# Router logits of 13 tiles as GpSimd products and ScalarE sums, all queries made with 512 columns in the normalisation stage

## The reference

```python
h = layernorm(x)
q, k, v = h @ W_q.T + b_q, h @ W_k.T + b_k, h @ W_v.T + b_v
z = (q @ k.T) / sqrt(512) * adj
z = where(z == 0, -10000, z)
x = x + relu(softmax(z, axis=1) @ v)
X = layernorm(x)
router_w = softmax(X @ Wr)                # Wr: 512 x 8
topk_w, topk_idx = top_k(router_w, 2)     # two of eight experts, weights softmax(topk_w)
x = x + swiglu(X, shared) + sum over the two experts of weight * swiglu(X, expert)
```

## Time and profile before

| | |
|---|---|
| time, median of 3 runs | 1431.06 us (1430.62 to 1432.37) |
| the profiled execution | 1431.42 us, its span 1429.3 us |
| granted TensorE clock, mean | 0.998 |
| TensorE (PE) busy | 1417.1 us, 99% |
| VectorE (DVE) busy | 672.1 us, 47% |
| ScalarE (ACT) busy | 438.1 us, 31% |
| GpSimd (POOL) busy | 188.9 us, 13% |

### The profile page before, as it was taken

The page is one execution under the profiler, slowest core; times in us unless marked ns, Lnnn a source line. Parts: engine busy times, 40 slices in busy tenths (PEclk is TensorE's granted clock), DMA queues, the critical chain, the costliest instruction groups (busy, mean ns, idle before and its releaser), DMA issues.

```text
span 1429.3 us, 19916 instructions
## 1 busy us (share of the span) xinstructions
PE 1417.1 (99%) x7140; PEld 1224.3 (86%) x7140; DVE 672.1 (47%) x1425; ACT 438.1 (31%) x705; POOL 188.9 (13%) x233
## 2 busy tenths in 40 slices
PE   8999999999999999999999999999999999999999
PEld 6788888888888888898999889898898989888887
DVE  4955656665666577543253425234152525242222
ACT  3521121222111235343243424234242525231211
POOL 1510111121112133011001010101101010100000
PEclk9999999999999999999999999999999999999999
DMA  4811222232213256272617134251435262621000
GB/s 145 247 58 65 99 72 73 73 99 85 81 66 118 73 178 235 89 213 54 197 31 214 29 74 156 44 200 34 117 109 151 78 160 86 183 88 60 0 30 30
DMA packets 81666, 149.81 MB, mean 105 GB/s; under 512 B 10464, under 2 KB 20704, under 8 KB 79536
## 3 DMA queue, kind: packets, MB, share of 16 engines
q1 hardware_dynamic: 65312, 117.76, 23.9%
q0 software_dynamic: 9760, 18.93, 6.7%
q10 hardware_dynamic: 6528, 12.22, 3.1%
HBM read 109.90 MB, written 40.04 MB: 105 GB/s over the span
## 4 chain that ended last, share of the span: by engine, by line
PE 98%; DVE 1%; DMA 0%; SPq 0%; issue 0%; POOL 0%; ACT 0%; DVEq 0%; POOLq 0%
PE bank L234 92%; PE bank L667 2%; PE bank L690 1%; PE bank L871 1%; PE bank L820 1%; PE bank L684 0%; DMA wk_raw<-in_L_gnn_W_k_dram 0%; PE bank L827 0%; PE bank L620 0%; PE bank L604 0%; SPq L312 0%; DVE y L1546 0%; PE bank L698 0%; PE bank L636 0%; DVE xn L1197 0%
## 5 line engine op out<-in xcount | busy, mean ns | idle before, releaser
L1514 DVE TENSOR_TENSOR hid<-bank,hid 128x384 f32<-128x384 f32 (+1 forms) x96 | 57.8, 602 | 355.6 <-PE bank L234 355.6
L234 PE MATMUL bank<-dn_h,hT_h 128*128 128x512 f32 x416 | 167.1, 402 | 0.3 <-DVE hT_l L1185 0.3
L234 PE MATMUL bank<-dn_h,hT_l 128*128 128x512 f32 x416 | 163.2, 392 | 0.0
L234 PE MATMUL bank<-dn_l,hT_h 128*128 128x512 f32 x416 | 162.8, 391 | 0.0
L234 PE MATMUL bank<-xq_h,gate_h 128*128 128x384 f32 (+1 forms) x384 | 136.2, 355 | 0.1
L234 PE MATMUL bank<-xq_h,gate_l 128*128 128x384 f32 (+1 forms) x384 | 136.1, 354 | 0.0
L234 PE MATMUL bank<-xq_l,gate_h 128*128 128x384 f32 (+1 forms) x384 | 135.7, 353 | 0.0
L234 PE MATMUL bank<-xq_h,up_h 128*128 128x384 f32 (+1 forms) x384 | 135.6, 353 | 0.0
L234 PE MATMUL bank<-xq_h,up_l 128*128 128x384 f32 (+1 forms) x384 | 135.4, 353 | 0.0
L234 PE MATMUL bank<-xq_l,up_h 128*128 128x384 f32 (+1 forms) x384 | 135.3, 352 | 0.0
L1089 ACT ACTIVATE hid<-bank 128x384 f32<-128x384 f32 (+1 forms) x96 | 50.7, 528 | 224.0 <-PE bank L234 224.0
(11 more groups left out here) (214 smaller groups left out, 2791.1 us busy)
## 6 DMA issues: line engine op xcount, KB each, us to landing
adj_t<-in_adj_dram SPq DMA_DIRECT2D x16, 1024.0 KB
gate_raw<-in_L_ffn_Wg_dram SPq DMA_DIRECT2D x16, 1024.0 KB, 5.4
up_raw<-in_L_ffn_Wu_dram SPq DMA_DIRECT2D x16, 1024.0 KB, 9.1
dn_raw<-in_L_ffn_Wd_dram SPq DMA_DIRECT2D x16, 1024.0 KB, 11.3
x_t<-in_x_dram SPq DMA_DIRECT2D x24, 256.0 KB, 4.3
slots<-x2row ACTq DMA_DIRECT2D x12, 512.0 KB, 4.3
e_x<-slots ACTq DMA_DIRECT2D x22, 256.0 KB, 2.7
acc<-x SPq DMA_DIRECT2D x16, 256.0 KB
```

What stands on the lines that cost most here:

```text
L234: mm = pe.matmul(o, lhs(a, c), rhs(b, c), start=first and n == 1, stop=last and n == 3 * len(chunks))
L1514: dve.tensor_tensor(hid[:, c % 2, 0:w], bank[2 + c % 2][:, 0:w], hid[:, c % 2, 0:w], ALU.mult).then_inc(sem("hid"), 1)
```

## The change

- The queries of all tiles are made in the normalisation stage, from its fourth tile on and during the first scores, in 16 blocks with 512 columns (`queries(q)`). ScalarE adds the bias (`keep_queries`; the scale is put into A), SyncE stores each to DRAM (`store_queries`), and in the loop the queries of the next pair are fetched in two halves into one tile `y_f` (`load_queries`), from which ScalarE and VectorE make the two parts. The second half is fetched when the first has been read.
- The router logits of tiles 1 to 13 (`BY_ROWS`) are made from the normalised row itself: for each expert GpSimd multiplies the row by a row of the transposed router weights (`products`, two buffers), and ScalarE sums the product (`sum_products`). The last three tiles use TensorE as before. The transposed weights are made by one DMA with single numbers as its pieces (`wrt`) near the start, and spread over all partitions later (`wr_rows`).
- The order within a step changes: the turned row behind the third score block, the count of picks one step later and behind the first score block, `pick_weights` and `ranks` of the tile before behind the second fill, `logits` behind the second half of the queries.
- adj is loaded in two halves; `sc` keeps eight pieces of 512 columns, which the two tiles use in turn; `x1`, `y_f` and others lie at new addresses. The last two steps are written out on their own (`step_before_last`, `last_step`).
- ScalarE's second SiLU of the experts waits until all rows of x1 are stored. Calls of `wait` with a positive value become direct `wait_ge`, and the setup semaphores are joined in one.

```diff
+    y_all = nc.dram_tensor("y_all", [T // 2, DC * 256], F32, kind="Internal").ap()
+    wrt = nc.dram_tensor("wrt", [E, D], F32, kind="Internal").ap()
...
-sc = at("sc", 168 * K, [P, 2, T])
+sc = at("sc", 168 * K, [P, 8 * 512])
+prod = at("prod", 180 * K, [P, 2, D])
+wr_rows = at("wr_rows", 128 * K, [P, E, D])
+y_new = at("y_new", 152 * K, [P, 2, 512])
 fill = at("fill", 184 * K, [P, 512])
-y_f = at("y_f", 186 * K, [P, 2, 256])
+y_f = at("y_f", 192 * K, [P, 2, 256])
 x_t = at("x_t", 188 * K, [P, 2, D])
-x1 = at("x1", 192 * K, [P, D])
+x1 = at("x1", 186 * K, [P, D])
...
+BY_ROWS = NT - 3
+def place(b, n, final=False):
+    return (4 + n if final or n < 2 else n) if b else n
+def whole(b, final=False):
+    return slice(place(b, 0, final) * 512, (place(b, 0, final) + 4) * 512) if final or not b else slice(1024, 3072)
 def queries_follow(j, b):
     return b == 0 and (not isinstance(j, int) or j + 1 < NT // 2)
+def logits_follow(i):
+    return not isinstance(i, int) or 1 <= i <= BY_ROWS
...
+    sp.dma_start(wrt, w_r.rearrange("d e -> e d"), allow_slow_non_contiguous=True).then_inc(sem("in_wr"), 16)
...
+    def store_queries(q):
+        g, m = q // 4, q % 4
+        sp.wait_ge(sem("y_kept"), q + 1)
+        sp.dma_start(y_all[2 * g * P:2 * (g + 1) * P, m * 256:(m + 1) * 256].rearrange("(a p) q -> p a q", p=P),
+                     y_new[:, q % 2, :].rearrange("p (a q) -> p a q", a=2)).then_inc(sem(f"y_out{q % 2}"), 16)
+    def load_queries(j, half):
+        wait(sp, "yT_l", 2 * j + half)
+        sp.dma_start(y_f[:], rows(y_all, j)[:, half * 512:(half + 1) * 512].rearrange("p (c q) -> p c q", c=2)
+                     ).then_inc(sem("y_in"), 16)
+    def load_adj(i, half):
+        wait(sp, "scored", 4 * i - 2 + 2 * half)
+        sp.dma_start(adj_t[:, half * 1024:(half + 1) * 1024], rows(adj, i)[:, half * 1024:(half + 1) * 1024]
+                     ).then_inc(sem(f"adj_in{half}"), 16)
     for t in range(4, NT):
         wait(sp, "ln1_done", t - 3)
         load_x(t)
-    wait(sp, "wv_turned", DC)
-    sp.dma_start(adj_t[:], rows(adj, 0)).then_inc(sem("adj_in"), 16)
+        if t >= 10:
+            store_queries(t - 10)
+    sp.wait_ge(sem("wv_turned"), DC)
+    load_adj(0, 0)
+    load_adj(0, 1)
...
+    load_queries(0, 0)
+    store_queries(6)
+    store_queries(7)
+    load_queries(0, 1)
+    for q in range(8, 16):
+        store_queries(q)
+    load_adj(1, 0)
+    sp.wait_ge(sem("y_kept"), 16)
+    sp.wait_ge(sem("in_wr"), 32)
+    sp.dma_start(wr_rows[:].rearrange("p e d -> p (e d)"),
+                 wrt.rearrange("(a e) d -> a (e d)", a=1).broadcast_to([P, E * D])).then_inc(sem("in_wr"), 16)
+    for half in range(2):
+        sp.wait_ge(sem(f"y_out{half}"), 16 * 8)
...
+    def store_row(i):
+        sp.wait_ge(sem("x1_done"), i + 1)
         sp.dma_start(rows(acc, i), x1[:]).then_inc(sem("x1_out"), 16)
-        wait(sp, "x2T_done", i + 1)
+    def store_turned(i):
+        sp.wait_ge(sem("x2T_done"), i + 1)
         sp.dma_start(rows(x2t, i), x2T[:].rearrange("p c q -> p (c q)")).then_inc(sem("x2t_out"), 16)
-    fetch(0, 0)
-    fetch(1, 1)
-    store(0)
+    def serve(j, b):
+        i = 2 * j + b
+        load_adj(i + 1, 1)
+        fetch(i, b)
+        ahead = queries_follow(j, b)
+        if ahead:
+            load_queries(j + 1, 0)
+        if not isinstance(i, int) or i > 0:
+            store_row(i - 1)
+        if not isinstance(i, int) or i + 2 < NT:
+            load_adj(i + 2, 0)
+        if not isinstance(i, int) or i > 0:
+            store_turned(i - 1)
+        if ahead:
+            load_queries(j + 1, 1)
+    serve(0, 0)
+    serve(0, 1)
     with sp.Fori(1, NT // 2 - 1) as j:
         for b in range(2):
-            fetch(2 * j + b, b)
-            store(2 * j + b - 1)
-    fetch(NT - 2, 0)
-    store(NT - 3)
+            serve(j, b)
...
+    serve(NT // 2 - 1, 0)
...
+    store_row(NT - 2)
+    store_turned(NT - 2)
+    sp.wait_ge(sem("attended"), 4 * NT)
     load_unit(1)
+    store_row(NT - 1)
     wait(sp, "xq_l", prepared(0))
-    wait(sp, "w_l", 2)
+    sp.wait_ge(sem("w_l"), 2)
     load_unit(2)
-    store(NT - 1)
...
+    def products(n, b):
+        wait_apart(pool, "x2_done", n)
+        for e in range(E):
+            wait_apart(pool, f"logit_sum{e % 2}", 4 * (n - 1) + e // 2)
+            pool.tensor_tensor(prod[:, e % 2, :], x2row[b][:], wr_rows[:, e, :], ALU.mult).then_inc(sem("products"), 1)
     power_of_row(1, 0)
+    pool.wait_ge(sem("in_wr"), 48)
+    products(1, 0)
     power_of_row(2, 1)
+    products(2, 1)
     scatter(1, 0)
-    with pool.Fori(1, NT // 2) as j:
+    with pool.Fori(1, BY_ROWS // 2) as j:
         power_of_row(2 * j + 1, 0)
+        products(2 * j + 1, 0)
         scatter(2 * j, 1)
         power_of_row(2 * j + 2, 1)
+        products(2 * j + 2, 1)
         scatter(2 * j + 1, 0)
+    power_of_row(BY_ROWS, 0)
+    products(BY_ROWS, 0)
+    scatter(BY_ROWS - 1, 1)
+    for n in range(BY_ROWS + 1, NT + 1):
+        power_of_row(n, (n - 1) % 2)
+        scatter(n - 1, n % 2)
...
-    def queries(j, half):
-        for c in range(2):
-            m = 2 * half + c
-            mm = product(pe, bank[7][:, c * 256:(c + 1) * 256], lambda a, d: A[a][:, d, m * P:(m + 1) * P],
-                         lambda b, d: xnT[b][:, d, bass.ds(j * 256, 256)], range(DC))
-        mm.then_inc(sem("y_ps"), 1)
+    def queries(q):
+        g, m = q // 4, q % 4
+        pe.wait_ge(sem("A_done"), DC)
+        pe.wait_ge(sem("xnT_l"), 4 * g + 4)
+        wait(pe, "y_kept", q - 1)
+        product(pe, bank[4 + q % 2][:], lambda a, d: A[a][:, d, m * P:(m + 1) * P],
+                lambda b, d: xnT[b][:, d, g * 512:(g + 1) * 512], range(DC)).then_inc(sem("y_ps"), 1)
...
-    def attention_step(j, b, last=False, prev=True, split=False):
+    def attention_step(j, b):
         i = 2 * j + b
...
+        prev = not isinstance(i, int) or i > 0
         if b == 1:
             wait(pe, "yT_l", 2 * j + 4)
         scores(i + 1, 1 - b, 0)
+        if not isinstance(i, int) or i > 1:
+            count_picks(i - 1)
         scores(i + 1, 1 - b, 1)
         turn(i, b, 0)
         turn(i, b, 1)
+        scores(i + 1, 1 - b, 2)
         if prev:
             turn_normalised(i, b)
-        scores(i + 1, 1 - b, 2)
-        if prev:
-            route_logits(i)
         scores(i + 1, 1 - b, 3)
-        ahead = queries_follow(j, b)
-        if ahead:
-            if prev:
-                wait(pe, "logits_read", i)
-            queries(j + 1, 0)
         attend(i, 0)
         turn(i, b, 2)
         attend(i, 1)
-        if ahead:
-            wait(pe, "yT_f", 2 * j + 3)
-            queries(j + 1, 1)
         turn(i, b, 3)
         attend(i, 2)
-        if split:
-            turn(i + 1, 1 - b, 0)
         attend(i, 3)
...
+        if t >= 3:
+            queries(t - 3)
         values(t)
...
+        act.wait_ge(sem("y_in"), 16 * n + 16)
+        wait(act, "scores", 4 * n if half == 0 else 4 * n - 4)
         copy(yT["h"][:, 2 * half:2 * half + 2, :], y_f[:]).then_inc(sem("yT_h"), 1)
...
+    def keep_queries(q):
+        act.wait_ge(sem("y_ps"), q + 1)
+        act.wait_ge(sem("bias_read"), 3)
+        wait(act, f"y_out{q % 2}", 16 * (q // 2))
+        act.activation(y_new[:, q % 2, :], bank[4 + q % 2][:], ACT.Identity, bias=c1[:, q % 4:q % 4 + 1]
+                       ).then_inc(sem("y_kept"), 1)
...
+    def sum_products(i, e0, e1):
+        for e in range(e0, e1):
+            wait(act, "products", E * (i - 1) + e + 1)
+            act.activation(prod[:, e % 2, :], prod[:, e % 2, :], ACT.Copy, accum_out=lg[:, e:e + 1]
+                           ).then_inc(sem(f"logit_sum{e % 2}"), 1)
+    def attention_step(j, b):
         i = 2 * j + b
+        prev = not isinstance(i, int) or i > 0
+        ahead = queries_follow(j, b)
         group(i, 0)
         group(i, 1)
...
-        if prev:
-            keep_turned(i)
-            router_exp(i)
-        ahead = queries_follow(j, b)
+            sum_products(i, 3, 5)
         if ahead:
             queries(2 * j + 2, 0)
-        if split:
-            first_pieces(0, 2)
+        if prev:
+            sum_products(i, 5, 7)
         group(i, 2)
-        if split:
-            probabilities(i + 1, 1 - b)
+        if prev:
+            sum_products(i, 7, 8)
+        if ahead:
+            queries(2 * j + 3, 1)
+        if prev:
+            router_exp(i)
+        group(i, 3)
+        probabilities(i + 1, 1 - b)
         if prev:
             pick_exp(i)
-        if ahead:
-            queries(2 * j + 3, 1)
...
+        if n == 1:
+            act.wait_ge(sem("x1_out"), 16 * NT)
         act.activation(hid[:, c % 2, 0:w], bank[c % 2][:, 0:w], ACT.Silu).then_inc(sem("silu"), 1)
...
-    def scaled_queries(n, half):
-        wait(dve, "y_ps", n + 1)
-        wait(dve, "yT_h", n)
-        wait(dve, "yT_l", n)
-        for c in range(2):
-            m = 2 * half + c
```

(40 more changed lines are left out.)

432 lines of the change are left out of this document (239 added, 193 removed).

## The result

The changed kernel takes 1484.73 us (median of 4 runs, 1481.28 to 1486.22) against 1430.84 us before in the same comparison: ratio 1.0374, 95% interval 1.0355 to 1.0394. It is slower by 54 us. I had forecast 1439 us, slower by 8, with a range to 1453. The profiled execution has a span of 1483.8 us, 54.5 more than before.

What follows compares the result with a forecast made beforehand. TensorE, busy 99% of the span, was taken as the bound. From 1431.4 us, less 13.9 of TensorE work, plus 20 of loop waits and 1.4 at the end, came 1438.9, say 1439 us; range 1416 to 1453.

Steps and rivals of the forecast that it cites:

- Work taken from TensorE: Attention loop and queries: router matmuls leave 13 tiles (12.0 us) and wider query matmuls save 1.9; 13.9 us less.
- Head: Start of kernel: the router weights' single-number DMA, queued ahead of the x tiles, delays x by 0 us, at most 8.
- The prediction's own sign of being wrong here: Start of kernel: the forecast is wrong if x4 stalls TensorE near 45 us.
- The port step in the loop: Attention loop: VectorE's two-input instructions wait up to 1.03 us for GpSimd products sharing their ports, 3.6 us per tile.
- the first rival: Attention loop: VectorE's fills escape the port waits, even steps keep 2.3 us slack; 1419 us, chance 0.31.
- The size of the waits: Attention loop: TensorE waits 2.8 to 5.4 us in each of six even steps; 20 us taken, bounds 0 and 32.
- Tiles between the waits: Attention loop: time from tile to tile alternates between 24.3 and some 27 to 28 us; fills' tensor_scalar mean near 1 us.
- GpSimd's loop: GpSimd per tile: power, row, products, scatter take 23.1 us, under TensorE's 24.3; port waits make it 24.5 to 25.5.
- my third rival: Attention loop: GpSimd bounds every tile, products 1.45 us or more, loop 26.5 or more; about 1455 us, chance 0.09.
- a sign of being wrong: Attention loop: the forecast is wrong if GpSimd's products are longer than 1.3 us.
- End: End of kernel: ScalarE's second SiLU waits for x1's last store, queued behind weights; 1.4 us, bounds 0 and 3.4.
- The rivals on the other side: Attention loop: port waits cost nothing (1419 us, chance 0.31) or under 2 us per even step (1424 to 1431, 0.18).

Runs made afterwards that it cites:

- turned: The changed kernel, but router weights are turned on the chip (TensorE transposes, ScalarE copy, store of eight rows) instead of by the single-number transfer; 1459.82 us.
- reordered: `turned`, but VectorE does the queries' first half, third group and mask before pick weights and ranks, and ScalarE copies the third group before the sixth sum; 1449.28 us.
- logits_on_te: `turned`, but TensorE makes the router logits of all tiles, with no GpSimd products or ScalarE sums; 1430.44 us.
- other_queue: The changed kernel, but the single-number transfer of router weights is issued by ScalarE on its own queue; 1479.46 us.
- first_half_early: `turned`, but VectorE subtracts the first half of the next queries before the pick weights and ranks; 1442.34 us.

## Why the prediction was wrong

- *Work taken from TensorE*: right. 13.9 forecast, 14.0 measured, from 0.86 per tile and 2.8 for the queries.
- *Head*: this step failed, and it is the largest miss, 26.6 of some 46 us. I wrote "I take 0, since short pieces are nearer to the row that landed without a trace; bound 8". A DMA of 512 pieces says little on one of 4096, and the bound took the mean packet of another queue for each number, spread over 16 engines. In the trace packets under 512 B rise by 4888; the transfer takes from 11 to about 50 us (1640 such packets from 20 to 30 us, 1284 to 40, 648 to 50, 75 to 60), and SyncE stands 21.4 us in the issue of the next x, which no term of mine had. The prediction's own sign of being wrong here, x4 stalling TensorE near 45 us, came true. The Trainium skill (DMA: Bandwidth & Descriptors, "Rules for kernel authors") has the transfer as one descriptor per element; the packet count agrees. Its other half, eight outer rows on at most eight engines, does not seem to hold here: 83.1% of 16 engines' time is more than eight can make with one packet at a time, though the trace does not name the engines. My estimate by it, x 35 us late, was still nearer than my own term.
- *The port step in the loop*: right in its mechanism. The two-input reduction (1.52 us against 0.69) and tiny instructions (1.12 against 0.16), which I had left open, wait as well; halving the length of a product takes away more than half of what they lose (the reduction's mean is 1.10, with halves 0.84 and 0.82, without products 0.69). So the first rival, that the fills slip through, is out. The Trainium skill's rule (SBUF — State Buffer, "SBUF: two separate sides") is what these rows show.
- *The size of the waits*: too small, 20 us against 35.4, and this step failed too: with the head mended (`turned`) the kernel takes 1459.8 us, still above my 1453. The path was right. In the step shown, which begins at 271.0, the fourth group is ready 26.5 us later; I had 24.4 (24.3, since 18.1 + 2.9 is 21.0 and not 21.1), or 2.6 more if the tiny instructions wait too, and they do. TensorE's waits, 25.7 in all, lie inside my 17 to 32, above the 20 that I took. They come as two per even step and not one, since the third group stands behind the ranks: I had followed only the fourth. And I did not price what TensorE does after a wait: in four of six even steps matmuls start 0.43 instead of 0.23 us apart, some 6 us in all.
- *Tiles between the waits*: odd steps take 24.1 to 25.2 us, as said; even ones 29 to 31, not 27 to 28. The fills' tensor_scalar has a mean of 0.72 us in the loop, not near 1, since the third and fourth fill come after the products.
- *GpSimd's loop*, 23.1 us forecast: a product takes 1.42 to 1.45 us, as in my third rival and beyond the 1.3 that I had named as a sign of being wrong. It decided nothing in the changed kernel, where each power waited for VectorE and none for a landing, and was the next bound as soon as the order was changed (`reordered`).
- *End*: 1.4 forecast, 4.7 measured. I took 1 us for the store behind the weights; it landed 11.6 us after its issue, 2.1 after the last of the three loads, and the SiLU waited 5.71 us. The count waited 3.1 us, and behind it TensorE ran at the lower clock, 1.4 us more, which I had not priced here either. With the store first, mark 3 to 4 is what it was before the change.

The rivals on the other side needed VectorE's delay to be below 2.3 us per even step. It was about 5 in the step shown: 0.23 + 0.83 + 0.90 + 0.82 in the fills, and 0.96 in the addition of the ranks, with 0.47 and 0.90 in two more small instructions beside it.

## What to carry to other kernels

Work moved to an idle engine is free only if that engine's instructions don't hold something that a busy neighbour needs: look at what the neighbour does in that stretch, and whether a fetch, an in-order queue or a reused buffer hangs on it. Here the same products are a gain in the steps in which VectorE has room and a loss in the others. And a transfer is priced by its pieces, not by its bytes: 16 KB in single numbers cost 25 us, almost as much as the products of 13 tiles, with their sums, cost on balance (29 us between `turned` and `logits_on_te`).

## What the runs showed of the hardware

- A transfer of 4096 single numbers took from 11 to about 50 us (1643 packets and 0.01 MB in 10 us, their times 83.1% of 16 engines). The engine that had issued it stood in its next DMA issue, SyncE for 21.4 us and ScalarE, in `other_queue`, for 28.8; a load on another queue landed 14.8 us after its issue instead of 2.9.
- A GpSimd product of 256 columns took 0.83 us beside VectorE, one of 512 columns 1.45 and one of 128 columns 0.51: by the first two, about 0.2 us of each do not go with its length.
- A wait of 2.46 us on TensorE was followed by nine matmuls at half pace (297.52 us), one of 2.01 us 5.5 us earlier by none (292.05 us). Neither the length of a wait nor its having another close before it decides: in `first_half_early`, which has no second wait, the pace fell after waits of 2.08 us (260.49) and 1.95 us (365.14) and not after one of 2.09 us (417.80). What decides is not shown. The loop's clock is 0.99 on average there and 0.97 in `turned`.
